# Unread products in TensorE's pauses, from the end of the first attention to the last experts

## The reference, cut to what matters

```python
x = x + L0_xattn(layernorm(x), ctx)   # 16 heads over 6272 context rows
x = x + L0_attn(layernorm(x))         # RWKV time mix and channel mix
x = x + L0_ffn(layernorm(x))          # 8 experts, top 2
x = x + L1_xattn(layernorm(x), ctx)   # 16 heads over 6272 context rows
x = x + L1_attn(layernorm(x))         # rotary attention over the 64 tokens
x = x + L1_ffn(layernorm(x))          # feed-forward on values rounded to 8 bits
x = x + L2_xattn(layernorm(x), ctx)   # keeps the 32 best of 6272 rows, S4D, feed-forward
x = x + L2_attn(layernorm(x))         # local attention over the 64 tokens
x = x + L2_ffn(layernorm(x))          # attention, then 8 experts in groups
x = x + L3_xattn(layernorm(x), ctx)   # 16 heads over 6272 context rows
x = x + L3_attn(layernorm(x))         # attention to the past
x = x + L3_ffn(layernorm(x))          # one shared expert and 8, top 2
```

## Time and profile before

| what | us |
|---|---|
| median of 3 runs (lowest, highest) | 662.75 (660.69, 663.55) |
| the profiled execution's own time | 660.76 |
| its span, first to last instruction | 658.9 |
| TensorE (matmul) busy | 510.0 |
| VectorE busy | 437.2 |
| ScalarE busy | 300.7 |
| GpSimd busy | 133.3 |
| TensorE's mean granted clock | 0.863 of 2.4 GHz |

### The profile page before, as it was taken

The page is one execution under the profiler, slowest core; times in us unless marked ns, Lnnn a source line. Parts: engine busy times, 40 slices in busy tenths (PEclk is TensorE's granted clock), DMA queues, the critical chain, the costliest instruction groups (busy, mean ns, idle before and its releaser), DMA issues. The chain is left out here.

```text
span 658.9 us, 12012 instructions
## 1 busy us (share of the span) xinstructions
PE 510.0 (77%) x4818; PEld 324.5 (49%) x4819; DVE 437.2 (66%) x851; ACT 300.7 (46%) x369; POOL 133.3 (20%) x199
## 2 busy tenths in 40 slices
PE   8989996788789996438994593772578488999756
PEld 4645663575255564313442263472556335556545
DVE  5764326746968955744999999925546596785243
ACT  2868882325566684111754560020112164768511
POOL 2211100000000000205698999300000000000000
PEclk9999997989999998556997688795569679999959
DMA  8544490753200000001022035051300150000000
GB/s 212 140 125 133 118 357 9 225 129 87 88 2 2 2 2 3 1 0 50 0 85 111 0 147 128 1 129 42 127 1 1 36 252 1 2 2 2 2 0 3
DMA packets 17258, 45.46 MB, mean 69 GB/s; under 512 B 4153, under 2 KB 13226, under 8 KB 16362
## 3 DMA queue, kind: packets, MB, share of 16 engines
q1 hardware_dynamic: 17076, 44.47, 22.4%
q0 software_dynamic: 128, 0.23, 0.1%
HBM read 34.28 MB, written 8.29 MB: 65 GB/s over the span
## 5 line engine op out<-in xcount | busy, mean ns | idle before, releaser
L251 POOL TENSOR_TENSOR rstd<-rstd,minus_half 64x1 f32<-64x1 f32 x20 | 11.8, 589 | 421.7 <-DVE rstd L259 421.7
L1531 ACT ACTIVATE ring<-psum,l3x_gain_columns 128x1024 f32<-128x1024 f32 x49 | 54.4, 1114 | 22.9 <-PE psum L1423 22.9
L1531 ACT ACTIVATE ring<-psum,l1x_gain_columns 128x1024 f32<-128x1024 f32 x49 | 54.4, 1114 | 22.4 <-PE psum L1423 22.4
L1437 PE MATMUL psum<-ring,values 128*32 128x128 f32 x1568 | 62.7, 279 | 0.4 <-ACT ring L1531 0.4
L944 ACT ACTIVATE ring<-psum,l0x_key_scale 128x1024 f32<-128x1024 f32 x49 | 52.4, 1114 | 9.9 <-PE psum L833 9.3
L1437 PEld LDWEIGHTS psum<-ring,values 128*32 128x32 f32 x1568 | 36.9, 109 | 28.1 <-issue 24.7
L1636 DVE TENSOR_REDUCE l3x_tops<-psum 128x1 f32<-128x448 f32 x64 | 36.7, 620 | 10.2 <-PE psum L1412 10.1
L1636 DVE TENSOR_REDUCE l1x_tops<-psum 128x1 f32<-128x448 f32 x64 | 36.7, 619 | 10.2 <-PE psum L1412 10.1
L3220 DVE MAX8 l2x_best<-values 128x8 f32<-128x6272 f32 x6 | 40.1, 6692 | 0.1
L3228 DVE MATCH_REPLACE8 values<-l2x_best,values 128x6272 f32<-128x6272 f32 x6 | 40.1, 6676 | 0.0
L1423 PE MATMUL psum<-l3x_Q_stack,wide 98*128 98x256 f16 x196 | 29.7, 275 | 2.1 <-DVE l3x_Q_stack L1595 1.3
(11 more groups left out here) (782 smaller groups left out, 1084.4 us busy)
## 6 DMA issues: line engine op xcount, KB each, us to landing
wide<-keys_aside SPq DMA_DIRECT2D x54, 224.0 KB, 3.7
experts<-in_experts SPq DMA_DIRECT2D x1, 4608.0 KB, 13.4
experts<-in_experts SPq DMA_DIRECT2D x1, 4096.0 KB, 15.8
keys_aside<-ring SPq DMA_DIRECT2D x7, 448.0 KB, 2.4
keys_aside<-experts SPq DMA_DIRECT2D x6, 448.0 KB, 2.6
ring<-in_ctx_tiles SPq DMA_DIRECT2D x1, 2352.0 KB, 9.7
experts<-in_experts SPq DMA_DIRECT2D x1, 2048.0 KB, 7.8
ctx_t<-in_ctx_t SPq DMA_DIRECT2D x3, 672.0 KB, 8.0
```

The costliest lines, as they stand in the source:

```text
L1437: last = nc.tensor.matmul(ps[32 * quarter:32 * quarter + 32, O_BANK, 128 * half:128 * half + 128], mem.values[:, at:at + 32], probs[:, t % ...
L1531: nc.scalar.activation(probs[:, t % PROBS, :].rearrange("p (b n) -> p b n", b=2), ps[:, pair:pair + 2, :], ACT.Exp, scale=exp_gain[:, :]). ...
```

## The change

A helper issues products of the tile of ones with itself into a PSUM bank that holds nothing needed, in pieces of up to 512 columns. It is called from 31 places, which makes 35 runs of it and 33,024 columns in all (two calls serve two stages each through `SmallHeads.pe`, one runs at levels 1 and 3, one at levels 0 and 3); a call stands in front of one of TensorE's waits or at the end of its list. Nobody reads the results, and nobody waits for them but by the order of TensorE's list and the meeting at the end of a block. Nothing is removed or moved. The default of `units` loses its fourth element, which is not used.

```diff
+def fill(mem, pe, columns, bank):
+    for lo in range(0, columns, 512):
+        n = min(512, columns - lo) // 128
+        mem.nc.tensor.matmul(mem.psum[:, bank, 0:n * 128], mem.ones[:, :],
+                             spread(mem.ones[:, :], 1, [128, n, 128]), start=True, stop=True)
...
 stage_first_attention
                 last.then_inc(*pe_done.mark("own"))
+                fill(mem, pe, 640, O_BANK)
...
                 last.then_inc(*pe_done.mark("projected"))
+                fill(mem, pe, 1408, O_BANK)
 stage_long_attention
+                if level == 3:
+                    fill(mem, pe, 1024, 1)
                 pe.wait_ge(*dve_done.at("xn"))
...
                 for n in late_values:
                     project("V", n)
+                if level == 3:
+                    fill(mem, pe, 1024, 1)
...
                 last.then_inc(*pe_done.mark("own"))
+                fill(mem, pe, 640, O_BANK)
 stage_rwkv
                 last.then_inc(*pe_done.mark("kv"))
+                fill(mem, pe, 256, 3)
 stage_topk_experts
+                fill(mem, pe, 896, 7)
                 pe.wait_ge(*dve_done.at("xn"))
 SmallHeads.pe
-    def pe(self, pe, v_event, between=(lambda count: None), units=(0, 0, 0, 0)):
+    def pe(self, pe, v_event, between=(lambda count: None), units=(0, 0, 0), fillers=(0, 0, 0)):
...
         between(units[0])
+        fill(mem, pe, fillers[0], 7)
         pe.wait_ge(*mem.dve_done.at("probs"))
...
         between(units[1])
+        fill(mem, pe, fillers[1], 7)
         pe.wait_ge(*mem.dve_done.at("PT"))
 stage_rope_attention
+                fill(mem, pe, 1024, 6)
                 pe.wait_ge(*dve_done.at("xn"))
...
                     .then_inc(*pe_done.mark("qkv"))
+                fill(mem, pe, 896, 6)
                 gains.pe_bounds(pe, 2)
                 mem.quantised.pe(pe, WEIGHT_BANKS)
                 pe.wait_ge(mem.quantised.copied, 4)
+                fill(mem, pe, 384, 6)
                 pe.wait_ge(*dve_done.at("rotated"))
...
                     .then_inc(*pe_done.mark("turned"))
-                heads.pe(pe, "rotated")
+                fill(mem, pe, 256, 6)
+                heads.pe(pe, "rotated", fillers=(2304, 640))
                 gains.pe_column(pe, 4)
+                fill(mem, pe, 384, 6)
                 pe.wait_ge(*dve_done.at("OT"))
 stage_quantised_ffn
+                fill(mem, pe, 1024, 3)
                 pe.wait_ge(*dve_done.at("xn"))
...
                 spread_top(0)
+                fill(mem, pe, 640, 3)
                 pe.wait_ge(*dve_done.at("xq"))
...
                 last.then_inc(*pe_done.mark("gate_up"))
+                fill(mem, pe, 640, 3)
                 pe.wait_ge(*dve_done.at("h"))
...
                 spread_top(1)
+                fill(mem, pe, 896, 3)
                 pe.wait_ge(*dve_done.at("hq"))
 stage_local_attention
+                fill(mem, pe, 2 * 512, 7)
                 pe.wait_ge(*dve_done.at("xn"))
...
                     .then_inc(*pe_done.mark("qkv"))
-                heads.pe(pe, "V", lambda count: early.pe(pe, count), (2, 1, 1))
+                fill(mem, pe, 512, 7)
+                heads.pe(pe, "V", lambda count: early.pe(pe, count), (2, 1, 1), (3 * 512, 512))
 stage_transformer_experts
+                fill(mem, pe, 2 * 512, 7)
                 pe.wait_ge(*dve_done.at("z"))
...
                 early.pe(pe, 2)
+                fill(mem, pe, 384, 7)
                 pe.wait_ge(*dve_done.at("mid"))
...
                 experts.pe_out(pe)
+                fill(mem, pe, 1408, 2)
 stage_past_attention
+                fill(mem, pe, 1024, 7)
                 pe.wait_ge(*dve_done.at("z"))
                 nc.tensor.transpose(ps[0:C, 0, 0:T], mem.xn[:, :], ident[0:T, 0:T]).then_inc(*pe_done.mark("zT"))
+                fill(mem, pe, 128, 7)
...
                     .then_inc(*pe_done.mark("scores"))
+                fill(mem, pe, 896, 7)
                 pe.wait_ge(*dve_done.at("probs"))
...
                     .then_inc(*pe_done.mark("out"))
+                fill(mem, pe, 384, 7)
 stage_topk_attention (its tail)
                 last.then_inc(*pe_done.mark("film"))
+                fill(mem, pe, 10 * 512, 3)
                 pe.wait_ge(*dve_done.at("film_out"))
                 nc.tensor.transpose(ps[0:T, 6, 0:C], mixed[:, :], ident).then_inc(*pe_done.mark("mixed"))
+                fill(mem, pe, 2 * 512, 3)
                 pe.wait_ge(*dve_done.at("h"))
...
                 last.then_inc(*pe_done.mark("hidden"))
+                fill(mem, pe, 512, 3)
                 pe.wait_ge(*act_done.at("hidden"))
...
                 last.then_inc(*pe_done.mark("out"))
+                fill(mem, pe, 2 * 512, 3)
```

## The result

The changed kernel takes 652.5 us (median of 4 executions, 651.6 to 655.4), the kernel before 661.8 in the same rounds (660.7 to 663.5). The ratio is 0.985, 95% interval 0.982 to 0.989: 9.3 us faster where I had forecast 19.8. It came out where the rival "held in part" stands (651).

The account below looks back on a forecast made before the run. Chains where engines take turns, with TensorE at half clock for 181 of 659 us, bound the kernel. Savings of 22.1 less 0.5 us, less 2.3 for two falls, gave −19.3 from 660.8: 642 us, range 637 to 647 (0.58).

Parts of the forecast that it names:

- held in part: Rival: four or five more clock falls at 2 us give back 9 us, 651 us (647 to 657.4); chance 0.23.
- prices of the short stages: Full-clock savings by product, such as eight-record products 0.82 us each, first experts 3.1 us, last experts 2.1 us.
- fourth cross-attention 3.0: Fourth cross-attention: 1.5 us off at L1351, 1.5 us off from first top score to first weighing.
- list of thin places: Transformer stage between first transpose and scores, and third cross-attention's start, stay thin; feed-forward's first maximum is near.
- the border: TensorE busy share dividing lost from held clock: 1.37 of 3.30 us lost it, 1.81 of 3.40 did not.
- What I wrote of level 1: Second cross-attention: first top score to first weighing takes 22.95 us, at full clock throughout, against level 3's 24.5.
- Two falls foreseen: Transformer stage and third cross-attention's start: two clock falls expected, costing 1 to 1.5 us each, 2.3 us in all.
- Border of first attention and RWKV: There the transposed state waits behind three early units at half clock; full clock takes 0.9 us off.
- What would show it: Signs: mean clock 0.93 or more, PEclk 1.00 from 99 to about 300, TensorE busy time up only some 20 us.
- Wrong in its premise if the level still falls at the borders: Failure sign: clock level still falling at the stage borders would refute the sum's premise.
- slower: Rival: additions run at low clock at stage borders, about 3.4 us a fall; at ten falls 673 us; chance 0.07.
- four passes: Lone float32 products of 64 columns behave like four passes, N = 256 in the skill's rule: 0.37 and 0.27 us.

Follow-up runs that it names:

- second comparison: Both kernels run once more, unedited: before 662.9 us (ratio 1.001), changed 650.9 us (0.983).
- experiment 8: Changed kernel with both long cross-attentions' loops filled, plus additions in RWKV, transformer stage and third cross-attention's start: 643.6 us (0.971), again 644.4 (0.970).
- experiment 2: Changed kernel with more unread products in the second and fourth cross-attentions, loops included, and at the first experts' end: 645.8 us (0.973).
- experiment 5: Changed kernel without its two 1024-column additions in the fourth cross-attention: 657.9 us (0.989).
- experiment 3: Changed kernel without the 640- and 1408-column additions at the end of the first cross-attention: 657.1 us (0.990).
- experiment 6: 1.6 us VectorE delay before the fourth cross-attention: kernel before 669.9 us (1.010), changed 648.3 (0.976), changed without that stage's two additions 655.3 (0.987).
- experiment 9: Changed kernel with only the fourth's loop filled 646.6 us (0.977), only the second cross-attention filled 650.4 (0.982); all places plus three more 643.9 (0.971).

## Why the prediction was wrong, point by point

By the medians 9.3 us (12.2 in the second comparison, 11.0 from profile to profile) stand against 19.8.

- **The prices of the short stages were right.** First experts 3.0 (forecast 3.1; against before's other profiles, where that stage took 19.3 and 19.2, only 1.6), last experts 2.2 (2.1), L2178 at 1.04 and 1.06 (1.09) in two stages, L2403 at 1.40 (1.45). The feed-forward gave 2.5 and the local attention 2.0; the prediction has no sums by stage to hold against these. The 5120 columns took 8.8 us and the product behind them waited 0.77 for VectorE, where I had them 0.7 inside their pause. L2171 (L2154 before), seen at half clock only when I took 0.45 off for it, takes 0.68 for 1.13 in the local attention, 0.45 off; in the rope stage it took 1.00, across a change of the level, and in the transformer stage still 1.13. At full clock there, in the second profile of experiment 8, it takes 0.67:

```profile
478.25 0.67 PE L2188 MATMUL psum<-l2f_KT,ring 32*128 32x64 f32 x16
```

- **The step that failed: "fourth cross-attention 3.0", and the list of thin places behind it.** I named two places where nothing is added and priced them at 2.3 us. I left out the top-score loops and the start of the weighing, where nothing is added either, and which are as thin. For the fourth's loop I even had the fall before my eyes: the low stretch of before at 536.0 lies between the two rows of level 3 in the earlier trace rows, and I took 1.5 us for its going, though the change puts nothing there:

```profile
535.96:542.78 6.82, 6.80 (x19) 2.53 (x20) 6.82 (x7) 3.45 (x4) 0.00 (x0) 0.50 0.21 90
```

The weighing I had at nothing. The fourth cross-attention in three parts, each from the timeline, in us:

| kernel | to the first top-score product | from it to the first weighing | from that to the end |
|---|---|---|---|
| before, both profiles | 9.4 | 24.5 | 76.0 |
| forecast (1.5 and 1.5 off) | 7.9 | 23.0 | 76.0 |
| changed, both profiles | 7.6 | 25.6 | 79.0 |
| loops filled (experiment 2) | 7.6 | 23.4 | 76.0 |
| without the two additions (experiment 5) | 9.4 | 27.2 | 79.0 |

So the start gave 1.9 where I had 1.5, the loop cost 1.15 where I had 1.5 off, and the weighing cost 3.0 where I had nothing: 2.3 us more in place of 3.0 less. In all seventeen profiles the last part takes 76.0 us without a low stretch at its start, and 79.0 to 79.4 in the seven that have one. The loop's price is that of late unread products: VectorE waits 2.98 us behind `keep_on` in the changed kernel, 0.84 in before and 0.63 with the loop filled. In before:

```profile
547.90 1.31 DVE L1595 CAST l3x_Q_stack<-psum 2x512 f16<-2x512 f32 x2 [0.84 <-PE psum L1393]
```

Fewer of these products would be the other cure; no run tried it.

The changed kernel before its falls at 533 and 161:

```profile
529.60:533.08 3.48, 2.05 (x10) 0.63 (x8) 3.48 (x4) 1.93 (x3) 0.00 (x0) 1.00 0.35 148
157.60:161.00 3.40, 1.85 (x17) 1.69 (x16) 0.96 (x3) 3.08 (x6) 0.00 (x0) 1.00 0.81 182
```

TensorE is busy 2.05 of 3.48 us and 1.85 of 3.40, more than the 1.81 of 3.40 in the earlier trace rows that lost nothing. So the busy share which I read as the border doesn't tell a fall from none. I had seen the second's loop at full clock in one profile of before and took this for its property. It was that execution's: in two others the second cross-attention had a fall in the loop. The fourth gave 3.5 us for the two additions (experiment 5) and lost more by its start's new place. With the loop filled it gave 3.0 against before, the forecast number by two errors that cancel: 1.9 and 1.1 for 1.5 and 1.5. 5.3 of the 8.3 us that the second profile lacks are this.
- **What I wrote of level 1.** It got no term. In seven profiles with the additions ahead of it the stage took 111.1, 111.7, 111.7, 112.5, 115.1, 117.3 and 117.3, mean 113.8; in five without them 111.1, 111.4, 112.5, 114.0 and 117.3, mean 113.3. Zero was right for the mean and 6 us wrong for the profile shown. In all three profiles at 117.3 the first fall came 1.4 to 1.5 us after the stage's start and two more followed in the loop; in the one at 114.0 it came at 1.4 too and none followed. The fall at the start costs 2.9 us (first top-score product at 15.1 us, for 12.2), the ones in the loop 3.3.
- **Two falls foreseen.** Both came (482 and 301). Start of the third cross-attention: right, the stage gained 1.5 and gains 1.1 to 1.2 more when held. Transformer stage: dearer, 1.9 us lost where I had at most 1.5, since the fall lasts 10.2 us and 56 records run in it; its L2178 came to 1.92, and was 1.78 before.
- **Border of first attention and RWKV**, 0.9: 1.6 in the mean of the profiles (experiment 3), none in the two compared first.
- **What would show it.** Clock 0.923, just under the 0.93 I asked for; the second profile has 0.936. PEclk dips five times between 99 and 300, not once. TensorE's busy time rose by 49 us, not 20: the additions took 62 (37.3 us on the tile of ones before, 99.1 after) and all else gave back 12, not 38, since half-clock products in the second cross-attention took the place of those in the short stages. With all places filled (experiment 8) it gave back 38. "Wrong in its premise if the level still falls at the borders" was the wrong test: it fell less at the borders, and more in the loops.
- **The rival "held in part"** had the number (651) and nearly the count (four or five more falls; seven in the first profile, five in the second), but only half of the mechanism: what cost most was no addition late behind a fall at a border. The dear falls lie where there are no additions; in the fourth's loop unread products were late all the same, the kernel's own.
- **Two readings.** The rival "slower" has the level falling at seven stage borders; in that profile six low stretches begin within about 3 us of one. And the "four passes" are a rough match: the formula quoted there gives 0.396 us for 256 columns at the low clock, where the row has 0.37.

## What to carry to other kernels

A stage's clock in one profile isn't a property of the stage. Before you price work on the clock, list every stretch in which TensorE waits for another engine by a regular pause, loops included, and see what unread products the kernel already has in front of its chain: at half clock they hold it up. Take two or three profiles; a stage that differs by several us between them at the same instructions is one of these. And if a stage's start moves, the stages behind it may change length by more than the move: read the gain stage by stage, and test with a plain delay.

## What the runs showed that I had not expected

The kernel's work alone doesn't fix the points at which the clock rises and falls. The same 1.6 us of idle VectorE work made one kernel 6.3 us slower and another 2.6 us faster, through where the falls lie against the fourth cross-attention's start. With the same program in that stage (but for 640 columns near its end) the first one began 1.40 us ahead of the start, or 0.04, 1.79, 2.67 or 3.16 us after it, and the stage took 116.2, 109.9, 115.7, 114.1 and 109.6 us: no even course, and the length goes by whether a low stretch meets the weighing. The Trainium skill (TensorE: Matmul & The Clock Gate, the part on the clock gate) says that what decides on the level runs freely, so that one kernel starts slowly for a different number of products from run to run. These profiles agree: of the first ten records of L292, which every kernel here has, four to six start at half clock. It prices that start at under 1% of a span and advises against fitting to a count of slow products. Here the difference goes on behind the start: one stage moved by 6 of 650 us, about that 1%, and the 56 executions of the kernel before lie between 660.7 and 670.3.

It is random only in part. In two pairs of profiles the clock first rose at nearly the same time, and each pair agrees, to 0.15 and 0.05 us, in every stage up to the first whose instructions differ. The first six records of L292, in the changed kernel's first profile and in experiment 5, then in its second profile and in experiment 6:

```profile
1.06 4.29 PE L292 MATMUL psum<-ones 128*128 128x512 f32 x6 [1.06 <-DVE minus_half L599]
1.05 4.35 PE L292 MATMUL psum<-ones 128*128 128x512 f32 x6 [1.05 <-DVE minus_half L599]
1.05 4.83 PE L292 MATMUL psum<-ones 128*128 128x512 f32 x6 [1.05 <-DVE minus_half L599]
1.05 4.84 PE L292 MATMUL psum<-ones 128*128 128x512 f32 x6 [1.05 <-DVE minus_half L599]
```

The second cross-attention took 117.29 and 117.26 in the first two, 111.74 and 111.73 in the last two. So profiles with a like first rise can be compared, but it must be very like: one more profile with the same instructions up to there (experiment 9, the fourth's loop alone), whose six records took 4.76 us, has 115.05. In the last pair, then, the delay alone stands between 112.2 and 109.2 in the fourth cross-attention.

The fourth, 360 us behind the second, is steadier: where the changed kernel has its falls there, it came out at 112.21, 112.22, 112.29 (experiment 3) and, with the second's loop filled, 111.5, with its first fall 22.2, 22.2, 22.4 and 20.6 us after its start. That earlier stages which run partly at half clock pull the executions together would explain this; it was only argued.
